# Attention output of a delta-rule block made 512 columns wide by two accumulating matmuls for each pair of heads

## The chip, the cores and the metric

The kernel runs on one core of one Trainium2 chip. The metric is device time in microseconds for one execution of the whole program. Five engines of the core work side by side, each through its own list of instructions in order, and meet at semaphores: PE multiplies matrices (its weight loads are listed apart, as PEld), DVE does vector work and transposes blocks of 32x32, ACT does activations and copies, POOL small memsets, copies and indirect transfers, SP issues transfers.

## The reference

A transformer block over 16 sequences of 512 tokens and 128 channels: layer norm with a modulation, a gated delta-rule attention with 8 heads of 16 channels, an output projection, then a mixture of 16 experts. The part that the change touches is one line of the chunked delta rule, with chunks of 32 tokens:

```python
def step(S, xs):
    q_i, k_i, u_i, w_i = xs
    attn_local = jnp.where(mask_strict, 0.0, q_i @ jnp.swapaxes(k_i, -1, -2))
    u_new = u_i - w_i @ S
    o_i = q_i @ S + attn_local @ u_new          # <- this line
    S = S + jnp.swapaxes(k_i, -1, -2) @ u_new
    return (S, o_i)
```

## The kernel before, in words

Four stages follow one another: setup, `stage_front` (projections, the delta rule, stores to DRAM), `stage_back` (filters, gates, output projection, routing) and the experts. The change is in `stage_front`.

`stage_front` walks over 26 rounds, `i` from -10 to 15, with 16 chunks of 32 tokens. A round works at several depths at once: `n = i+9` normalizes and turns the input, `t = i+5` projects k, v, q and the gates, `t4 = i+4` scales, `t3 = i+3` makes the in-chunk attention, and `d = i` runs the recurrence. So rounds 0 to 6 have all of it, rounds 7 to 10 no `n`, round 11 has `t4`, `t3` and `d`, round 12 `t3` and `d`, rounds 13 to 15 only `d`. Each engine has one list for all rounds, written out by hand and fully unrolled, and `need(engine, semaphore, n)` puts a wait into it.

The 128 partitions hold four quads of 32. A quad and a sequence make a pair of heads, so there are 64 such pairs, and `per_pair` (L562) issues one 32x32 matmul for each. PE's order in a round is: `r` (L596, state times scaled keys), the gates' spread `sm` (L600), half of k's projection, `gl` (L608), the other half, `u` (L617), half of v, `ga` (L624), half of v, `s` (L632, the state), half of q, `o1` (L639, q times state), half of q, the two fusion matmuls `f0` and `f1` (L646), `o` (L649, attention times u), the input's transposes `x` (L655) and the `dense` group (L659 to L666).

`o1` and `o` both write `ps_b`, 64 columns for each pair: the two heads of a pair beside each other, 32 tokens each, and all 32 channels of the pair for both. For head 0 only the first 16 channels mean something, for head 1 only the last 16. DVE turns all 1024 columns (L795) into `o_wide`, which is the buffer of `u_wide`; ACT's `take_valid` (L443) copies the valid halves in two activations into `o_tok`, and SP stores that (L414). The same `take_valid` makes `u_tok` from `u_wide` (L493).

What stands after the second `take_valid` in ACT's list is the modulated input `f_hT` (L552) and the copy `f_dense` (L558), and the next round's `sm` on PE waits for `f_dense`. What stands around L795 in DVE's list is the triangular solve (`part`, L681 and L684), the transposes of its result (L804, two of them in odd rounds), and then `r` of the next round (L702), `f_sm_tok` (L708) and `L` (L732); PE's `u` waits for L702 and L732.

Of the kernel before, what the change touches and what calls it, by code (L numbers as in the profile page):

```python
# [19 lines left out]
ACT = mybir.ActivationFunctionType  # L20
AXX = mybir.AxisListType.X

P = 128
NB, S, D = 16, 512, 128
NH, DH = 8, 16
C = 32
# [6 lines left out]
NQ, G2 = 4, 2  # L33
# [246 lines left out]


FIRST = -10
D_K, D_Q, D_KT, D_W, D_KG, D_T, D_A = 3, 6, 6, 5, 5, 4, 4


def need(eng, sem, n, per=1):

    if n >= 0:
        eng.wait_ge(sem, (n + 1) * per)  # L289


def unit(n):

    return n if 0 <= n < NCH else None


def stage_front(nc, g, a):


    with ExitStack() as stack:  # L300
        k = Ctx(nc, stack)
        W = NB * C
# [6 lines left out]
        q_cm = [k.sb(f"f_q_cm{u}", [P, W]) for u in range(D_Q)]  # L309
# [17 lines left out]
        TT = [TT_all[:, u, :, :, :] for u in range(D_T)]  # L327
        attn = [k.sb(f"f_attn{u}", [P, NI, C]) for u in range(D_A)]
        r = k.sb("f_r", [P, W])
        u_wide, u_tok = k.sb("f_u_wide", [P, NB * 64]), k.sb("f_u_tok", [P, W])  # L330
        o_wide = u_wide
        state = [k.sb(f"f_state{u}", [P, W]) for u in range(2)]
        o_tok = [k.sb(f"f_o_tok{u}", [P, W]) for u in range(2)]
        ps_p = [k.ps(f"ps_p{u}") for u in range(2)]
# [4 lines left out]
                   v_halo k_turned v_turned short_step short_done s_turned sm_turned sm_halved  # L339
                   nk_root nk_inv beta_ready bn_step gamma_ready kg_turned kg_ready w_ready heads_ready  # L340
                   gl_ps ga_ps L_taken attn_ready L_masked solved TT_ready
                   state_ready r_ps r_ready u_ps u_ready u_copied s_ps o1_ps o_ps o_turned o_copied fir_ready""".split()
        s = {n: nc.alloc_semaphore(name="f_" + n) for n in names}
        xs_in = [nc.alloc_semaphore(name=f"f_xs_in{u}") for u in range(3)]
        v_out, s_out, sm_out, o_out = ([nc.alloc_semaphore(name=f"f_{n}_out{u}") for u in range(2)] for n in ("v", "s", "sm", "o"))
# [1 line left out]
        quad = lambda q: slice(32 * q, 32 * q + 32)  # L347
        by_seq = lambda x: x.rearrange("p (b c) -> p b c", b=NB)
        SOLVE = 60
        every_TT = TT_all[:, :, :, :, :].rearrange("p t b i g -> p (t b i g)")  # L350
        window = every_TT[:, NB * D:].rearrange("p (c w k) -> p c w k", c=C, w=2)
        w_in = nc.alloc_semaphore(name="f_w_in")
        own.append(w_in)
        block = stack.enter_context(nc.Block())
# [29 lines left out]
        @block.sync  # L384
        def _(sp):
            def load_x(n):
                need(sp, s["xh_ready"], n - 3)
                sp.dma_start(x_in[n % 3][:, :, :], a.x[4 * (n % 4):4 * (n % 4) + 4, n // 4 * P:n // 4 * P + P, :]
                             .rearrange("b p d -> p b d")).then_inc(xs_in[n % 3], 16)

            def store(dst, t, src, sems):
                sp.dma_start(dst[t], src).then_inc(sems[t % 2], 16)

            for n in range(3):
                load_x(n)
            for q in range(NQ):
                sp.dma_start(window[quad(q), :, :, :], a.windows[q]).then_inc(w_in, 16)
            for i in range(FIRST, NCH):
                m = unit(i + 4)
                if m is not None:  # L400
                    need(sp, s["s_turned"], m)
                    store(a.s_tok, m, s_tok[m % 2][:, :], s_out)
                    need(sp, s["sm_halved"], m)
                    store(a.logits, m, sm_half[m % 2][:, :, :].rearrange("p b r -> p (b r)"), sm_out)
                t = unit(i + 5)
                if t is not None:
                    need(sp, s["v_turned"], t)
                    if t >= 3:
                        store(a.v_tok, t, v_of(t), v_out)
                n = unit(i + 12)  # L410
                if n is not None and n >= 3:
                    load_x(n)
                if unit(i) is not None:
                    need(sp, s["o_copied"], i)  # L414
                    store(a.o_tok, i, o_tok[i % 2][:, :], o_out)
            for sems in (s_out, sm_out, o_out):
                for sem in sems:
                    sp.wait_ge(sem, 16 * NCH // 2)
            for u, n in ((0, 6), (1, 7)):
                sp.wait_ge(v_out[u], 16 * n)  # L420

        @block.gpsimd
        def _(pool):
            pool.memset(state[1][:, :], 0.0).then_inc(s["state_ready"], 1)
            for i in range(FIRST, NCH):
                t, n = unit(i + 5), unit(i + 9)
                if t is not None:
                    need(pool, s["short_done"], t - 2)
                    if t == 0:
                        pool.memset(v_pad[0][:, :, 0:FIR_S - 1], 0.0).then_inc(s["v_halo"], 1)  # L430
                    else:
                        need(pool, s["silu_v"], t - 1)
                        pool.tensor_copy(v_pad[t % 2][:, :, 0:FIR_S - 1], v_pad[1 - t % 2][:, :, C:]).then_inc(s["v_halo"], 1)  # L433
                if n is not None:
                    j, rows = n // 4, slice(4 * (n % 4), 4 * (n % 4) + 4)
                    need(pool, s["dense_ps"], 4 * j - 5)
                    if j == 0:
                        pool.memset(hT[0][:, rows, 0:TAPS - 1], 0.0).then_inc(s["halo_ready"], 1)
                    else:
                        need(pool, s["h_ready"], n - 4)  # L440
                        pool.tensor_copy(hT[j % 2][:, rows, 0:TAPS - 1], hT[1 - j % 2][:, rows, P:]).then_inc(s["halo_ready"], 1)

        @block.scalar  # L443
        def _(act):
            def take_valid(out, wide):

                for n in range(G2):
                    last = act.activation(by_seq(out[:, :])[:, :, n * DH:(n + 1) * DH],
                                          by_seq(wide[:, :])[:, :, 48 * n:48 * n + DH], ACT.Copy)
                return last  # L450

            def upper_to_identity(half):
# [8 lines left out]
            for i in range(FIRST, NCH):  # L461
# [28 lines left out]
                if unit(i) is not None:  # L490
                    need(act, s["u_ready"], i)
                    need(act, s["o_ps"], i - 1)
                    take_valid(u_tok, u_wide).then_inc(s["u_copied"], 1)  # L493
                if n is not None:
                    need(act, s["ln_ready"], n)
                    need(act, s["x_ps"], n - 1)
# [40 lines left out]
                if t3 is not None:  # L537
                    need(act, s["L_taken"], t3)
                    upper_to_identity(L[t3 // 2 % 2][:, t3 % 2, :, :]).then_inc(s["L_masked"], 1)
                if unit(i) is not None:  # L540
                    need(act, s["o_turned"], i)
                    if i >= 2:
                        act.wait_ge(o_out[i % 2], 16 * (i // 2))
                    take_valid(o_tok[i % 2], o_wide).then_inc(s["o_copied"], 1)
                if n is not None:
                    need(act, s["x_ps"], n)
                    need(act, s["dense_ps"], 4 * (n // 4) - 5)
# [13 lines left out]
        def _(pe):  # L561
# [8 lines left out]
            double = lambda x: lambda b, q: x[quad(q), b * 64:b * 64 + 64]  # L570
            every = lambda b: True
            never = lambda b: False
            in_bank = lambda b: b % 8 == 0

            def u_pair(b, q):

                cols = u_wide[quad(q), b * 64:b * 64 + 64]
                return bass.AP(cols.tensor, cols.offset, [list(cols.ap[0]), [48, 2], [1, DH]])

            def project(t, kind, which, half):  # L580
                ps = free_bank(pe, kind, t) if half == 0 else ps_p[bank[kind, t]]
# [8 lines left out]
            for i in range(FIRST, NCH):  # L590
# [45 lines left out]
                if d is not None:  # L636
                    need(pe, s["attn_ready"], min(d + 3, NCH - 1))
                    need(pe, s["o_turned"], d - 1)
                    per_pair(double(ps_b), narrow(state[(d - 1) % 2]),  # L639
                             lambda b, q: q_cm[d % D_Q][quad(q), b * C:b * C + C].unsqueeze(1).broadcast_to([32, G2, C]), in_bank, stop=False)\  # L640
                        .then_inc(s["o1_ps"], 1)
                if t is not None:
                    project(t, "q", 0, 1)
                    for m in range(2):
                        ps = free_bank(pe, f"f{m}", t)
                        pe.matmul(ps[:, :], g.fus_W1[:, m * P:(m + 1) * P], tokens(t, TAPS - 1), start=True, stop=True).then_inc(s[f"f{m}_ps"], 1)  # L646
                if d is not None:
                    need(pe, s["u_copied"], d)
                    per_pair(double(ps_b), narrow(u_tok), lambda b, q: attn[d % D_A][quad(q), 2 * b:2 * b + 2, :].rearrange("p g c -> p (g c)"), never)\  # L649
                        .then_inc(s["o_ps"], 1)  # L650
                if n is not None:
                    ps = free_bank(pe, "x", n)
                    need(pe, s["xh_ready"], n)
# [16 lines left out]
        def _(dve):  # L670
# [18 lines left out]
            for i in range(FIRST, NCH):  # L689
# [66 lines left out]
                if d is not None:  # L756
                    need(dve, s["u_ps"], d)
                    need(dve, s["s_ps"], d - 1)
                    need(dve, s["u_copied"], d - 1)
                    need(dve, s["o_copied"], d - 1)  # L760
                    dve.transpose(u_wide[:, :].rearrange("p (b g z) -> p b g z", b=NB, g=G2), ps_a[:, :].rearrange("p (b i g) -> p b g i", b=NB, g=G2)).then_inc(s["u_ready"], 1)
                part(0, 3)
                if t3 is not None:
# [25 lines left out]
                part(10, 13)  # L789
                if d is not None:  # L790
                    need(dve, s["o_ps"], d)
                    need(dve, s["o_copied"], d - 1)
                    need(dve, s["s_ps"], d)
                    need(dve, s["u_copied"], d)
                    dve.transpose(o_wide[:, :], ps_b[:, :]).then_inc(s["o_turned"], 1)  # L795
                part(13, 15)
                if i % 2 == 1:
                    for m in (i + 1, i + 2):
# [680 lines left out]
```

## Time and profile before

| | |
|---|---|
| median of 3 runs | 1112.25 us (1108.51 to 1112.86) |
| the profiled execution | 1113.23 us, span 1111.5 us |
| mean granted TensorE clock | 0.852 of full |
| PE busy | 805.0 us, 72% of the span |
| weight loads busy | 497.9 us |
| DVE busy | 739.3 us, 67% |
| ACT busy | 461.1 us, 41% |
| POOL busy | 202.2 us, 18% |

Times on the page and in the rows are microseconds unless marked ns. A matmul of f32 shows as two MATMUL records and two LDWEIGHTS records, so a group of 64 pairs is "x128" of each. "Idle before, releaser" says what ended an engine's idle time; "issue" is time in which nothing that the profile shows kept the engine. The granted clock is a share of full speed.

### The profile page before, as it was taken

To read this page: it belongs to the slowest core of one execution; us is meant where nothing else is said; L and a number is where in the kernel's file an instruction comes from. 1 tells how busy PE (TensorE), PEld (TensorE's weight loads), DVE (VectorE), ACT (ScalarE), POOL (GpSimd) and SP (SyncE) were. 2 spreads that over 40 slices of the span, in tenths; PEclk is the share of its full clock that TensorE was granted. 3 is DMA by queue.
4 is the path that set the end of the run, shared out by engine and by line. 5 is a ranking of instruction groups with operands and counts; after the bars stand their busy time and mean duration, and the time that the engine had idled before them with its cause. 6 is when DMAs were issued, how large, how long until landed. Compare 5 with 4: busy or idle time off the path is not lost. (4 is left out here: it accounts for less than half of the span.)

```text
span 1111.5 us, 40970 instructions
## 1 busy us (share of the span) xinstructions
PE 805.0 (72%) x18289; PEld 497.9 (45%) x18289; DVE 739.3 (67%) x1595; ACT 461.1 (41%) x880; POOL 202.2 (18%) x227
## 2 busy tenths in 40 slices
PE   1388977989899899998655474989877156667660
PEld 1134434555455555555654473545532024444440
DVE  3143998889999899998886139899985524222320
ACT  1587665556556565554210113557566111001000
POOL 2000000000000000000000000111111057888875
PEclk9999997989999899999776766888888569778775
DMA  5200111011000101111000092344352024344432
GB/s 118 54 30 29 36 35 36 31 42 47 32 33 32 37 28 37 37 37 37 14 14 13 22 288 76 105 120 120 100 130 58 21 80 96 68 69 84 72 37 25
DMA packets 86440, 66.13 MB, mean 60 GB/s; under 512 B 18504, under 2 KB 72952, under 8 KB 86264
## 3 DMA queue, kind: packets, MB, share of 16 engines
q1 hardware_dynamic: 73580, 54.42, 17.2%
q0 software_dynamic: 11264, 8.40, 5.6%
q8 instruction: 144, 2.36, 0.9%
q10 hardware_dynamic: 1420, 0.70, 0.2%
q14 instruction: 32, 0.26, 0.1%
HBM read 36.33 MB, written 27.15 MB: 57 GB/s over the span
## 5 line engine op out<-in xcount | busy, mean ns | idle before, releaser
L586 PE MATMUL ps_p<-f_hT,Wconv 128*128 128x512 f32 x384 | 193.5, 634 | 3.3 <-ACT f_hT L552 1.6
L684 DVE TENSOR_TENSOR f_L<-f_L,f_prod 128x60 f32<-128x60 f32 (+14 forms) x240 | 121.3, 505 | 8.2
L681 DVE TENSOR_TENSOR f_prod<-f_L 128x60 f32<-128x60 f32 (+14 forms) x240 | 118.9, 495 | 6.0
L1299 POOL DMA_INDIRECT out_dram<-y,slot_row x64 | 101.1, 1580 | 27.8 <-issue 18.0
L586 PEld LDWEIGHTS ps_p<-f_hT,Wconv 128*128 128x128 f32 x384 | 70.3, 196 | 77.8 <-issue 70.0
L1348 ACT ACTIVATE act_g<-pe_g 128x512 f32<-128x512 f32 x32 | 17.4, 595 | 167.3 <-PE pe_g L1326 140.6
L433 POOL COPY f_v_pad<-f_v_pad 128x32 f32<-128x32 f32 x15 | 4.7, 311 | 418.3 <-ACT f_v_pad L515 418.3
L1316 PE MATMUL pe_x<-ident,got 128*128 128x128 f32 x64 | 15.5, 388 | 85.4 <-DMA got<-xh_dram,slot_row 85.4
L1290 POOL DMA_INDIRECT got<-xh_dram,slot_row x64 | 62.8, 982 | 57.8 <-POOLq L1179 38.6
L1377 DVE SCALAR_TENSOR_TENSOR y<-pe_y,slot_w,gb_rows 128x128 f32<-128x128 f32 x64 | 18.0, 345 | 81.7 <-DMA out_dram<-y,slot_row 74.2
L566 PE MATMUL ps_a<-f_TT,f_r 32*32 32x64 f32 x2048 | 41.9, 249 | 29.7 <-DVE f_L L732 18.0
L566 PEld LDWEIGHTS ps_a<-f_TT,f_r 32*32 32x32 f32 x2048 | 38.8, 128 | 39.3 <-issue 27.4
L1338 PE MATMUL pe_y<-w,gu 128*128 128x128 f32 x256 | 50.8, 381 | 7.2 <-DVE gu L1369 4.1
L1316 PEld LDWEIGHTS pe_x<-ident,got 128*128 128x128 f32 x64 | 10.2, 193 | 98.7 <-DMA got<-xh_dram,slot_row 97.0
L1338 PEld LDWEIGHTS pe_y<-w,gu 128*128 128x128 f32 x256 | 49.2, 295 | 8.9 <-DVE gu L1369 5.4
L1022 PE MATMUL b_ps_o<-b_WoB,b_nT 128*32 128x128 f32 x512 | 21.7, 322 | 32.7 <-DVE b_nT L1171 32.7
L1002 PE MATMUL b_ps_y<-b_v_rest,fir 32*32 32x64 f32 x768 | 42.5, 286 | 2.5 <-issue 2.5
L922 POOL TENSOR_SCALAR b_rstd<-b_mv 128x4 f32<-128x4 f32 x16 | 8.8, 548 | 189.1 <-DVE b_mv L1151 189.1
L566 PE MATMUL ps_b<-f_q_cm,f_state 32*32 32x64 f32 x2048 | 37.0, 223 | 7.9 <-issue 6.8
L1003 PE MATMUL b_ps_y<-b_v_rest,fir 32*32 32x64 f32 x768 | 42.5, 284 | 0.0
L566 PEld LDWEIGHTS ps_b<-f_q_cm,f_state 32*32 32x32 f32 x2048 | 32.8, 110 | 18.1 <-issue 16.8
L566 PE MATMUL ps_b<-f_attn,f_u_tok 32*32 32x64 f32 x2048 | 35.8, 224 | 6.4 <-issue 6.3
(247 smaller groups left out, 1792.2 us busy)
## 6 DMA issues: line engine op xcount, KB each, us to landing
w<-in_L_ffn_w_dram SPq DMA_DIRECT2D x48, 128.0 KB
f_x_in<-_attn_hidden_states_dram SPq DMA_DIRECT2D x16, 256.0 KB, 2.9
s_tok_dram<-f_s_tok SPq DMA_DIRECT2D x16, 256.0 KB, 2.1
o_tok_dram<-f_o_tok SPq DMA_DIRECT2D x16, 256.0 KB, 2.1
b_s_in<-s_tok_dram SPq DMA_DIRECT2D x16, 256.0 KB, 2.9
b_o_in<-o_tok_dram SPq DMA_DIRECT2D x16, 256.0 KB, 3.1
b_x_in<-_attn_hidden_states_dram SPq DMA_DIRECT2D x64, 64.0 KB, 2.0
out_dram<-b_x SPq DMA_DIRECT2D x64, 64.0 KB, 1.8
```

Source lines behind the costliest of these rows:

```text
L566: last = pe.matmul(out(b, q), lhs(b, q), rhs(b, q), start=start(b), stop=stop, skip_group_check=True)
L586: last = pe.matmul(ps[:, :], g.Wconv[:, which, tap, :], tokens(t, tap), start=(tap == 0), stop=(tap == TAPS - 1))
L681: dve.tensor_tensor(tmp, M[:, :, m + 1:, m:m + 1].broadcast_to([P, 2, rows, cols]), M[:, :, m:m + 1, 0:cols].broadcast_to([P, 2, rows, col ...
L684: dve.tensor_tensor(M[:, :, m + 1:, 0:cols], M[:, :, m + 1:, 0:cols], tmp, ALU.add).then_inc(s["solved"], 1)
L1002: pe.matmul(out, g.fir[quad(q), c, 1, :], now, start=True, stop=False, skip_group_check=True)
L1003: last = pe.matmul(out[:, 64 - n:], g.fir[quad(q), c, 0, :], past, start=False, stop=True, skip_group_check=True)
L1022: last = pe.matmul(ps_o[m % 2][quad(b % 4), b // 4 * D:(b // 4 + 1) * D], nT[m % 2][:, b * C:(b + 1) * C], WoB[:, b, :], start=False, stop ...
L1290: pool.indirect_dma_start(got[t % AHEAD][:, n * D:(n + 1) * D], None, flat_xh, bass.IndirectOffsetOnAxis(ap=g.slot_row[:, t, n:n + 1], axi ...
L1299: pool.indirect_dma_start(flat_out, bass.IndirectOffsetOnAxis(ap=g.slot_row[:, t, n:n + 1], axis=0), y[t % 2][:, n * D:(n + 1) * D], None, ...
L1316: last = pe.transpose(ps_x[:, n * P:(n + 1) * P], got[t % AHEAD][:, n * D:(n + 1) * D], g.ident[:, :])
L1338: last = pe.matmul(ps_y[:, n * D:(n + 1) * D], gu[:, m, n * P:(n + 1) * P], w3[u][:, m, :], start=(m == 0), stop=(m == 1))
L1377: last = dve.scalar_tensor_tensor(y[t % 2][:, n * D:(n + 1) * D], ps_y[:, n * D:(n + 1) * D], g.slot_w[:, t, n:n + 1], g.gb_rows[:, n // 2 ...
```

## The change

The output is made 512 columns wide. `o1` multiplies each pair's block-diagonal state once by q (32 columns instead of 64). `u` is copied into a zeroed buffer `u_apart` with one 32-channel block for each head of a pair, in which the other head's channels stay zero; `o` is then two matmuls of 32 columns for each pair, which accumulate. That makes 128 matmuls of `o` in place of 64; they are split in two halves, one behind `f0`, one behind `f1`. DVE turns the 512 columns straight into `o_tok`; ACT's second `take_valid` and its wait for `o_turned` go, SP waits for `o_turned`, and DVE now waits itself until the store from that `o_tok` has landed. DVE's L761 no longer waits for `o_copied`. POOL zeroes `u_apart` once at the start. The buffers of `f_TT` go from four to two; the window data of the filters, which was kept in two of them for a time, now lies in these two.

```diff
-D_K, D_Q, D_KT, D_W, D_KG, D_T, D_A = 3, 6, 6, 5, 5, 4, 4
+D_K, D_Q, D_KT, D_W, D_KG, D_T, D_A = 3, 6, 6, 5, 5, 2, 4
...
-        u_wide, u_tok = k.sb("f_u_wide", [P, NB * 64]), k.sb("f_u_tok", [P, W])
-        o_wide = u_wide
+        u_wide, u_apart = k.sb("f_u_wide", [P, NB * 64]), k.sb("f_u_apart", [P, G2, NB, C])
...
-        window = every_TT[:, NB * D:].rearrange("p (c w k) -> p c w k", c=C, w=2)
+        window = every_TT.rearrange("p (c w k) -> p c w k", c=C, w=2)
...
-                    need(sp, s["o_copied"], i)
+                    need(sp, s["o_turned"], i)
                     store(a.o_tok, i, o_tok[i % 2][:, :], o_out)
...
+            pool.memset(u_apart[:, :, :, :], 0.0).then_inc(s["zeroed"], 1)
...
-            def take_valid(out, wide):
+            def to_own_half(out, wide):
                 for n in range(G2):
-                    last = act.activation(by_seq(out[:, :])[:, :, n * DH:(n + 1) * DH],
-                                          by_seq(wide[:, :])[:, :, 48 * n:48 * n + DH], ACT.Copy)
+                    cols = slice(n * DH, (n + 1) * DH)
+                    last = act.activation(out[:, n, :, cols], by_seq(wide[:, :])[:, :, 48 * n:48 * n + DH], ACT.Copy)
...
-                if unit(i) is not None:
-                    need(act, s["o_turned"], i)
-                    if i >= 2:
-                        act.wait_ge(o_out[i % 2], 16 * (i // 2))
-                    take_valid(o_tok[i % 2], o_wide).then_inc(s["o_copied"], 1)
...
+            def own_attention(d, first, end):
+                for b in range(first, end):
+                    for n2 in range(G2):
+                        for q in range(NQ):
+                            last = pe.matmul(ps_b[quad(q), b * C:b * C + C], u_apart[quad(q), n2, b, :], attn[d % D_A][quad(q), 2 * b + n2, :],
+                                             start=False, stop=(n2 == 1), skip_group_check=True)
+                if end == NB:
+                    last.then_inc(s["o_ps"], 1)
...
-                    per_pair(double(ps_b), narrow(state[(d - 1) % 2]),
-                             lambda b, q: q_cm[d % D_Q][quad(q), b * C:b * C + C].unsqueeze(1).broadcast_to([32, G2, C]), in_bank, stop=False)\
-                        .then_inc(s["o1_ps"], 1)
+                    per_pair(narrow(ps_b), narrow(state[(d - 1) % 2]), narrow(q_cm[d % D_Q]), at_first, stop=False).then_inc(s["o1_ps"], 1)
...
+                    if d is not None:
+                        need(pe, s["u_copied"], d)
+                        own_attention(d, NB // 2 * m, NB // 2 * (m + 1))
...
-                    need(dve, s["o_copied"], d - 1)
-                    need(dve, s["s_ps"], d)
-                    need(dve, s["u_copied"], d)
-                    dve.transpose(o_wide[:, :], ps_b[:, :]).then_inc(s["o_turned"], 1)
+                    if d >= 2:
+                        dve.wait_ge(o_out[d % 2], 16 * (d // 2))
+                    dve.transpose(o_tok[d % 2][:, :], ps_b[:, 0:W]).then_inc(s["o_turned"], 1)
```

## Rows read from the trace of the kernel before

**Rows 1.** The page: DMA queues (packets, MB, share of 16 engines).
```profile
q8 instruction: 144, 2.36, 0.9%
```

**Rows 2.** Windows by stage: us, then busy us (count) of PE, PEld, DVE, ACT, POOL, granted clock, DMA.
```profile
174.57:376.20 201.63, 184.97 (x5640) 109.90 (x5640) 178.96 (x363) 116.74 (x238) 2.75 (x12) 0.94 0.11 38
376.20:523.96 147.76, 140.21 (x4677) 84.98 (x4677) 139.22 (x249) 84.44 (x162) 1.27 (x4) 1.00 0.10 34
523.96:639.20 115.24, 66.35 (x3456) 61.97 (x3457) 69.65 (x117) 16.05 (x47) 0.02 (x1) 0.72 0.05 17
...
243.51:275.22 31.71, 29.21 (x941) 17.63 (x941) 28.47 (x59) 19.94 (x41) 0.41 (x2) 1.00 0.11 35
```

**Rows 3.** Timeline at the end of round 3: start, us, engine line op, [idle before, releaser].
```profile
296.93 1.24 DVE L795 STREAM_TRANSPOSE f_u_wide<-ps_b 128x1024 f32<-128x1024 f32 x1
298.20 0.72 ACT L448 ACTIVATE f_o_tok<-f_u_wide 128x256 f32<-128x256 f32 x2 [3.15 <-DVE f_u_wide L795]
...
300.20 0.60 ACT L558 ACTIVATE f_dense<-ps_p 128x512 f32<-128x512 f32 x1
...
300.95 1.95 PE L600 MATMUL ps_p<-f_dense,spread 128*128 128x512 f32 x2 [3.40 <-ACT f_dense L558]
...
302.94 0.72 DVE L708 STREAM_TRANSPOSE f_sm_tok<-ps_p 128x512 f32<-128x512 f32 x1 [0.80 <-PE ps_p L600]
...
304.23 0.18 DVE L712 RECIPROCAL f_rstd<-f_dev 128x4 f32<-128x4 f32 x1 [0.58 <-ACT f_dev L474]
```

**Rows 4.** Groups by line: busy us, mean ns, then idle before.
```profile
L795 DVE STREAM_TRANSPOSE f_u_wide<-ps_b 128x1024 f32<-128x1024 f32 x16 | 19.9, 1244 | 19.8 <-PE ps_b L566 19.8
...
L728 DVE STREAM_TRANSPOSE f_s_tok<-f_short 128x512 f32<-128x512 f32 x16 | 11.4, 711 | 0.6
...
L448 ACT ACTIVATE f_o_tok<-f_u_wide 128x256 f32<-128x256 f32 x32 | 11.6, 410 | 67.1 <-DVE f_u_wide L795 67.1
```

**Rows 5.** Timeline of PE in round 4.
```profile
316.91 1.29 PE L566 MATMUL ps_s<-f_u_wide,f_k_tok 32*32 32x32 f32 x128
...
320.37 1.56 PE L586 MATMUL ps_p<-f_hT,Wconv 128*128 128x512 f32 x3 [1.55 <-issue]
...
326.25 1.98 PE L646 MATMUL ps_p<-f_hT,fus_W 128*128 128x512 f32 x4
328.16 1.99 PE L566 MATMUL ps_b<-f_attn,f_u_tok 32*32 32x64 f32 x128
```

**Rows 6.** Windows from one "issue" stall of PE to the next, rounds 12 to 15.
```profile
562.95:566.70 3.75, 1.99 (x129) 1.83 (x129) 3.54 (x7) 0.00 (x0) 0.00 (x0) 1.00 0.02 4
...
sum 26.31, PE 14.22 PEld 12.99 DVE 12.88 ACT 0.72 POOL 0.00; mean PE 2.03 PEld 1.86 DVE 1.84 ACT 0.10 POOL 0.00
```

**Rows 7.** Windows of round 8, cut after every 256 instructions of PE's list.
```profile
441.07:444.52 3.45, 3.45 (x142) 2.11 (x135) 2.84 (x6) 2.32 (x4) 0.00 (x0) 1.00 0.02 5
444.52:447.93 3.41, 3.41 (x150) 2.12 (x140) 3.27 (x8) 1.56 (x4) 0.22 (x1) 1.00 0.22 82
447.93:453.47 5.54, 5.54 (x142) 3.06 (x134) 5.23 (x10) 2.36 (x3) 0.00 (x0) 1.00 0.01 3
453.47:456.89 3.42, 3.42 (x143) 1.85 (x133) 3.32 (x5) 2.43 (x9) 0.00 (x0) 1.00 0.02 5
```

**Rows 8.** Timeline, rounds 11 to 15: what PE's `u` waits for, and DVE and ACT there.
```profile
547.27 1.02 PE L566 MATMUL ps_a<-f_heads_k,f_k_cm 32*32 32x64 f32 x57 [0.79 <-issue]
...
549.80 1.23 DVE L732 STREAM_TRANSPOSE f_L<-ps_a 128x1024 f32<-128x1024 f32 x1
...
551.28 0.97 PE L566 MATMUL ps_a<-f_TT,f_r 32*32 32x64 f32 x28 [2.99 <-DVE f_L L732]
...
574.97 1.29 PE L566 MATMUL ps_a<-f_TT,f_r 32*32 32x64 f32 x40 [3.35 <-DVE f_r L702]
...
599.95 1.29 PE L566 MATMUL ps_a<-f_TT,f_r 32*32 32x64 f32 x40 [7.19 <-DVE f_r L702]
...
634.90 0.72 ACT L448 ACTIVATE f_o_tok<-f_u_wide 128x256 f32<-128x256 f32 x2 [9.10 <-DVE f_u_wide L795]
```

More of the change, by code:

```diff
@@ L341, in stage_front @@
                    gl_ps ga_ps L_taken attn_ready L_masked solved TT_ready
-                   state_ready r_ps r_ready u_ps u_ready u_copied s_ps o1_ps o_ps o_turned o_copied fir_ready""".split()
+                   state_ready r_ps r_ready u_ps u_ready u_copied zeroed s_ps o1_ps o_ps o_turned fir_ready""".split()
         s = {n: nc.alloc_semaphore(name="f_" + n) for n in names}
@@ L492, in _ @@
                     need(act, s["o_ps"], i - 1)
-                    take_valid(u_tok, u_wide).then_inc(s["u_copied"], 1)
+                    need(act, s["zeroed"], 0)
+                    to_own_half(u_apart, u_wide).then_inc(s["u_copied"], 1)
                 if n is not None:
@@ L572, in _ @@
             never = lambda b: False
-            in_bank = lambda b: b % 8 == 0
+            at_first = lambda b: b == 0
             def u_pair(b, q):
@@ L638, in _ @@
                     need(pe, s["o_turned"], d - 1)
-                    per_pair(double(ps_b), narrow(state[(d - 1) % 2]),
-                             lambda b, q: q_cm[d % D_Q][quad(q), b * C:b * C + C].unsqueeze(1).broadcast_to([32, G2, C]), in_bank, stop=False)\
-                        .then_inc(s["o1_ps"], 1)
+                    per_pair(narrow(ps_b), narrow(state[(d - 1) % 2]), narrow(q_cm[d % D_Q]), at_first, stop=False).then_inc(s["o1_ps"], 1)
                 if t is not None:
                     project(t, "q", 0, 1)
-                    for m in range(2):
+                for m in range(2):
+                    if t is not None:
                         ps = free_bank(pe, f"f{m}", t)
                         pe.matmul(ps[:, :], g.fus_W1[:, m * P:(m + 1) * P], tokens(t, TAPS - 1), start=True, stop=True).then_inc(s[f"f{m}_ps"], 1)
[L647 to L650, printed above, removed]
+                    if d is not None:
+                        need(pe, s["u_copied"], d)
+                        own_attention(d, NB // 2 * m, NB // 2 * (m + 1))
                 if n is not None:
@@ L791, in _ @@
                     need(dve, s["o_ps"], d)
-                    need(dve, s["o_copied"], d - 1)
-                    need(dve, s["s_ps"], d)
-                    need(dve, s["u_copied"], d)
-                    dve.transpose(o_wide[:, :], ps_b[:, :]).then_inc(s["o_turned"], 1)
+                    if d >= 2:
+                        dve.wait_ge(o_out[d % 2], 16 * (d // 2))
+                    dve.transpose(o_tok[d % 2][:, :], ps_b[:, 0:W]).then_inc(s["o_turned"], 1)
                 part(13, 15)
```

## The prediction, made before the changed kernel ran

> **What bounds the kernel now.** I read the windows by stage first, then the end of one round on all engines, then PE alone.
>
> The stretch that the change touches runs from the first `u` of the recurrence to the start of the back stage. It has three parts [rows 2]: rounds 0 to 5, 33.6 us each (201.63 over 6); rounds 6 to 10, 29.55 us each (147.76 over 5); and a tail of 115.24 us, rounds 11 to 15 and the way out. In the first two parts PE is busy 92 and 95% and DVE 89 and 94%. Two in-order lists, both nearly full, wait for each other in a ring, so a gain on one counts only as far as the other allows. In the tail both are half idle, and the time is a chain.
>
> The end of round 3 shows how the ring costs PE time [rows 3]. ACT stands 3.15 us idle until DVE comes to L795, behind the solve. Then follow the copies into `f_o_tok`, `f_hT`, `f_dense`, and only then `sm`, which has left PE idle for 3.40 us. DVE in turn waits 0.80 us at L708 for `sm`, which here ran at a low clock (1.95 us). The granted clock over rounds 0 to 5 is 0.94, over round 2 alone 1.00, and round 2 is 1.9 us shorter than the mean of the six [rows 2].
>
> PE alone shows a second limit, and this decides my forecast. In the tail it stops for "issue" again and again, and from one such stop to the next lie 256 of its instructions (128 matmul records, 128 weight loads) each time: seven such windows take 26.31 us, 3.76 each, with 2.03 us of matmul in them [rows 6]. The instruction queue moved 144 packets in 2.36 MB, 16 KB each [rows 1]. I read this as code that comes in pages of 256 instructions; two page starts in a row lie 3.76 us apart when PE has nothing else to wait for. In full rounds a page is hidden when other work fills it. In round 8 the pages of the second half take 3.45, 3.41, 5.54 and 3.42 us [rows 7], with no stall; in round 4, stalls of 1.55 us and less do show [rows 5].
>
> **The change part by part.** *Matmuls.* `o1` turns from 64 to 32 columns: 1.99 becomes 1.29, the duration of `s` in that shape [rows 5], so -0.70 us. `o` becomes two such groups, 2.58 for 1.99: +0.59. The fusion pair (1.91 us from its start to that of `o`) is cut in two, which adds one change between full-size and small matmuls; no row shows a pair cut so. Between 0 (the pair without overhead) and 0.3 I take 0.2. PE's arithmetic therefore stays as it is, +0.1 us a round.
>
> *Instructions.* 64 more matmuls are 128 more records and 128 weight loads: exactly one more page in each of 16 rounds, all of it in the second half of the round, where pages already came at 3.4 us.
>
> The Trainium skill (Runtime: NRT & Kernel Launch, section Instruction fetch mechanics) says that code is refilled in 16 KiB blocks of 256 instructions while the current one runs, and that crossing a boundary is "mostly hidden". The block size agrees with this trace (2.36 MB in 144 packets); that it is hidden does not hold in the tail, where 1.7 us of 3.76 are idle. By the page the new block would cost nothing, which is the second rival below.
>
> *ACT.* The second `take_valid` (2 x 0.41 us) and the wait for L795 go [rows 4]. What is late next on that chain is `dense` on PE, which is done before `r`; so `sm` follows `r` at once, and PE's idle stretches of up to 3.4 us and the low clock behind them go. `f1` is later by half of `o`, and its gelu with it; that is hidden, because `dense` comes behind the other half.
>
> *DVE.* L795 turns half the columns: 1244 to 711 ns [rows 4], -0.53 a round. Its waits for `sm` (0.80) shrink. The new wait for the store two rounds back is hidden: that store was issued two rounds earlier. SP's wait changes its semaphore only, and what stands behind it is the next round's stores. POOL's memset stands at the head of a list that is busy for 4 us of these three parts [rows 2]; its first reader comes ten rounds later. The wait of `f_TT` for `u` two chunks back asks for what DVE has consumed by then at L761. These I take at 0; the TT wait would cost up to the 2.4 us of two L804s in each second round if that were wrong.
>
> **The sum, by stage.**
>
> *Rounds 0 to 5.* Round 2, without low clock, has PE busy for 29.2 us [rows 2]. To that come 0.1 and the stalls of the extra page. The pages of the second half (3.41, 5.54, 3.42, so 12.4 us [rows 7]) become four pages, which at 3.76 are 15.0: +2.6, or at 3.4 (the shortest that shows no stall) 13.6, +1.2; I take 2.0. PE then needs 31.3. DVE is busy 29.8 a round (178.96 over 6); less 0.53, plus what lies between its 60 instructions (363 over 6 rounds; 0.03 us each is my estimate from neighbouring starts, 1.8 together) and the 0.58 us that L712 waits for ACT [rows 3], which stays, it needs 31.7. Odd rounds have two L804s (2.4 us) and even ones none, and the ring takes the longer at each turn, so I add 0.4: 32.1 against 33.6, -1.5 a round, **-9 us**. Bounds: -1.9 a round if DVE's sum alone counts (-11), -0.5 if PE's stalls come on top of DVE's odd rounds (-3).
>
> *Rounds 6 to 10.* There is little idle time to win back. PE is busy 28.0 of 29.55 us, and the extra page adds 1.2 to 2.6; less the small stalls that exist I take +1.7 a round, **+8.5 us**. Bounds: -0.5 (DVE's shorter transpose alone, -2.5 in all) to +2.6 (+13).
>
> *Tail.* Here the page is bare, 3.76 us in each round, unless DVE hides it. Round 11: `gl` ends at 548.29 and `L` can be turned from 549.80, so 1.5 are hidden [rows 8]: +2.25. Round 12: PE then waits 3.35 us until L702 has run, of which some 0.7 is L702 itself; `r` therefore comes late by 3.76 - 2.6: +1.15. Round 13: PE waits 7.19 us for DVE, which hides the page, and DVE is 0.53 shorter: -0.5. Round 14 waits for nothing but code (0.79 us for L702 itself, behind `r`): +3.76. Round 15: +3.76. At the way out the 0.53 and the last copy (0.72) go: -1.25. Together **+9.2 us**; bounds +5 (pages at 3.4, more of it hidden) and +13 (nothing hidden in rounds 11 and 12).
>
> Back stage and experts are not touched. Sum: -9 + 8.5 + 9.2 = +8.7. The profiled execution took 1113.23 us (1.7 of it around the span); the median of the runs is 1 us below. I forecast 1121 us beside that median, own range 1114 to 1129.
>
> **Rivals.** *The page is hidden (faster).* Place: the second half of each round. If a page can start less than some 3.0 us after the one before it as soon as PE has work, 12.4 us hold four pages and no stall comes. Then rounds 0 to 5 give -1.9 each (-11), rounds 6 to 10 -0.5 each (-2.5), and the tail -1.25 and -0.5: -15, so 1097 us. For it: page starts 3.41 apart without a stall [rows 7]. Against it: seven windows in a row at 3.76 [rows 6], and a stall in round 4 in just this place, where one page holds `s` and half of q [rows 5]. The quoted page of the skill speaks for this rival; the rows of the tail speak against it.
>
> *A balance.* Gain and loss cancel: rounds 0 to 5 at -1.9, rounds 6 to 10 at +0.2 (the stalls lie under DVE's own work), tail +9: -11 + 1 + 9 = -1, so about 1111 us. For it: DVE and PE are so close that a small shift decides which one is late.
>
> *The clock falls.* With three pages of `o` in a row PE works some 2.2 us of each 3.76. In the tail the granted clock is 0.72 over all [rows 2], and 1.00 in a window of 3.75 us with 1.99 us of matmul [rows 6]. Should it fall from 2.4 to 1.2 GHz behind `o`, `x` and `dense` (2.4 us) take twice as long in 11 rounds: +26, so about 1147 us. Against it: it stayed at 1.00 in windows as thin as this.
>
> **How the numbers follow.** Forecast 0.52, page hidden 0.18, balance 0.22, clock 0.08. A measurement of this kernel tells about 0.5% from no change, 5.6 us: below 1106.7 is faster, above 1117.8 slower. Of the forecast 0.08 lies below that upper line, of the hidden page 0.02 above the lower one. Slower: 0.44 + 0.08 = 0.52; same: 0.22 + 0.08 + 0.02 = 0.32; faster: 0.16. The range of 1106 to 1133 holds the forecast and the balance and leaves out most of the hidden page and the clock, 0.2 together.
>
> **What would show it.** PE's idle time before `sm` by `f_dense` gone in rounds 0 to 6, and ACT no longer idle by L795. Rounds 0 to 5 near 32 us, 6 to 10 near 31, the tail near 124. Between `f0` and `r`, "issue" stalls of 1 to 2 us in every round, 256 instructions apart; 160 packets of code instead of 144. The prediction is wrong if the groups behind `f0` follow each other without such stalls, if rounds 6 to 10 don't grow, or if rounds 14 and 15 grow by less than 3 us each.

## The result, and the profile after

The changed kernel takes 1124.31 us (median of 4 runs, 1118.85 to 1127.85) against 1110.38 us for the kernel before on the same chip: a ratio of 1.0126, 95% interval 1.0069 to 1.0183. It is slower by 14 us (by the interval 8 to 20), where 1121 against 1112.25 (+9) was forecast, and inside the range.

The three parts of the front stage in the profiled execution of the changed kernel, from its first `u` to the start of the back stage (columns as in rows 2):

```profile
174.01:368.44 194.43, 177.90 (x6408) 106.87 (x6409) 174.97 (x362) 115.05 (x228) 2.57 (x12) 0.99 0.12 38
368.44:528.26 159.82, 142.14 (x5317) 85.16 (x5318) 138.40 (x250) 80.19 (x150) 1.65 (x4) 1.00 0.10 33
528.26:650.60 122.34, 68.65 (x4097) 64.22 (x4098) 67.22 (x117) 12.38 (x37) 0.04 (x1) 0.60 0.05 17
```

Beside [rows 2]: rounds 0 to 5 went from 201.63 to 194.43 us (-7.2), rounds 6 to 10 from 147.76 to 159.82 (+12.1), the tail from 115.24 to 122.34 (+7.1). Together +12.0. The part behind, which the change does not touch, took 472.3 us in the profile of before and 466.1 here; over the nine profiles of this study it lies between 466 and 476, so a single span says little about 6 us, and the windows say it better. Of the four executions the profiled one was the fastest, 1118.85 us.

PE's waits at lines of the front stage, over the whole execution, first of the kernel before, then of the changed one (who waited, for what: us in all, times, longest):

```profile
PE ps_p L600 <- ACT f_dense L558: 17.7, 12, 3.4
PE ps_b L566 <- issue: 13.1, 12, 1.9
PE ps_r L566 <- issue: 10.0, 6, 2.2
```
```profile
PE ps_b L581 <- issue: 29.7, 21, 2.2
...
PE ps_b L562 <- issue: 12.3, 12, 2.2
PE ps_r L562 <- issue: 12.1, 11, 2.2
...
PE ps_p L606 <- ACT f_dense L554: 3.6, 4, 1.0
```

That is the exchange in these lines: 14 us of waiting for `f_dense` gone (what is left, 3.6 us, lies ahead of the first `u`), 31 us of "issue" come. L566 holds `o1` and `o` together; of its 13.1 us 6.3 were at `o`, so the new `o` (L581) has 23 of the 31. With the smaller groups PE's "issue" waits grow by 9.2 us in rounds 0 to 5 (3.0 to 12.2), by 11.3 in rounds 6 to 10 (4.1 to 15.4) and by 14.6 in the tail (23.7 to 38.3). In rounds 0 to 5 the `f_dense` waits that went were 12.9 us; that these rounds are shorter all the same goes with PE's busy time, 177.90 us for 184.97, at a granted clock of 0.99 for 0.94.

The gain is seen at the end of round 3 of the changed kernel, first on PE, then on ACT, where [rows 3] had `sm` 3.40 us late:

```profile
293.57 1.09 PE L562 MATMUL ps_r<-f_state,f_kg_cm 32*32 32x32 f32 x105 [0.22 <-issue]
294.59 1.13 PE L606 MATMUL ps_p<-f_dense,spread 128*128 128x512 f32 x2
295.55 1.88 PE L592 MATMUL ps_p<-f_hT,Wconv 128*128 128x512 f32 x4
```
```profile
291.22 1.51 ACT L548 ACTIVATE f_hT<-ps_p,mod 128x128 f32<-128x128 f32 x4 [1.34 <-PE ps_p L659]
293.07 0.60 ACT L554 ACTIVATE f_dense<-ps_p 128x512 f32<-128x512 f32 x1 [0.35 <-PE ps_p L670]
```

ACT is never behind DVE here: `f_dense` waits only for PE, `sm` follows `r` at once and runs at full clock (1.13 us at a granted 1.00, for 1.95 at 0.53).

The loss is seen in round 9, on PE alone:

```profile
476.04 1.17 PE L562 MATMUL ps_b<-f_q_cm,f_state 32*32 32x32 f32 x114 [0.43 <-issue]
477.14 1.99 PE L592 MATMUL ps_p<-f_hT,Wconv 128*128 128x512 f32 x4
478.97 1.02 PE L651 MATMUL ps_p<-f_hT,fus_W 128*128 128x512 f32 x2
479.92 1.29 PE L581 MATMUL ps_b<-f_attn,f_u_apart 32*32 32x32 f32 x128
481.14 1.13 PE L651 MATMUL ps_p<-f_hT,fus_W 128*128 128x512 f32 x2
482.20 0.26 PE L581 MATMUL ps_b<-f_attn,f_u_apart 32*32 32x32 f32 x6
483.26 1.24 PE L581 MATMUL ps_b<-f_attn,f_u_apart 32*32 32x32 f32 x122 [0.80 <-issue]
...
486.73 1.90 PE L670 MATMUL ps_p<-f_hid,small_w 128*32 128x512 f32 x4 [1.25 <-issue]
488.56 1.24 PE L562 MATMUL ps_r<-f_state,f_kg_cm 32*32 32x32 f32 x123
490.84 0.25 PE L562 MATMUL ps_r<-f_state,f_kg_cm 32*32 32x32 f32 x5 [1.04 <-issue]
```

PE stops inside a group (after 6 of 128 records of `o`, after 123 of 128 of `r`), with nothing to wait for by its program. The starts behind these stops, 476.04, 483.26, 486.73 and 490.84, have 512, 256 and 256 instructions between them: 7.22 us for two pages, then 3.47 and 4.11 for one each. The times of the single packets in the trace tie these stops to code: a 16 KB packet of the instruction queue ends 1.2 us before the start at 483.26 and 1.4 us before those at 486.73 and 490.84. In [rows 7] the pages of this half of a round held 3.41 to 5.54 us of matmul and none of them stopped PE. The page of the profile now counts 160 packets of code:

```profile
q8 instruction: 160, 2.62, 1.0%
```

### The profile page after: what moved, and what is told of

The parts are those of the page before. It is cut to its first block and busy times, and to the rows that moved or that the text cites. A ratio compares the mean times of both kernels' runs of the same rounds, so it can differ in the third digit from the quotient of the medians.

```text
span 1116.7 us, 44992 instructions
## 1 busy us (share of the span) xinstructions
PE 797.5 (71%) x20337; PEld 495.6 (44%) x20337; DVE 731.6 (66%) x1595; ACT 451.0 (40%) x848; POOL 202.6 (18%) x228
## 5 line engine op out<-in xcount | busy, mean ns | idle before, releaser
L592 PE MATMUL ps_p<-f_hT,Wconv 128*128 128x512 f32 x384 | 187.1, 616 | 4.0 <-issue 2.2
L592 PEld LDWEIGHTS ps_p<-f_hT,Wconv 128*128 128x128 f32 x384 | 68.0, 190 | 74.1 <-issue 66.6
L581 PE MATMUL ps_b<-f_attn,f_u_apart 32*32 32x32 f32 x4096 | 50.9, 206 | 29.7 <-issue 29.7
L581 PEld LDWEIGHTS ps_b<-f_attn,f_u_apart 32*32 32x32 f32 x4096 | 45.5, 118 | 48.9 <-issue 48.9
L449 ACT ACTIVATE f_u_apart<-f_u_wide 128x256 f32<-128x256 f32 x32 | 11.6, 408 | 122.9 <-DVE f_u_wide L764 122.9
L1318 PEld LDWEIGHTS pe_x<-ident,got 128*128 128x128 f32 x64 | 10.5, 197 | 98.8 <-DMA got<-xh_dram,slot_row 97.0
L1024 PE MATMUL b_ps_o<-b_WoB,b_nT 128*32 128x128 f32 x512 | 21.7, 322 | 30.8 <-DVE b_nT L1173 30.7
```

Source lines behind the costliest of these rows:

```text
L581: last = pe.matmul(ps_b[quad(q), b * C:b * C + C], u_apart[quad(q), n2, b, :], attn[d % D_A][quad(q), 2 * b + n2, :], start=False, stop=(n ...
L592: last = pe.matmul(ps[:, :], g.Wconv[:, which, tap, :], tokens(t, tap), start=(tap == 0), stop=(tap == TAPS - 1))
L1024: last = pe.matmul(ps_o[m % 2][quad(b % 4), b // 4 * D:(b // 4 + 1) * D], nT[m % 2][:, b * C:(b + 1) * C], WoB[:, b, :], start=False, stop ...
L1318: last = pe.transpose(ps_x[:, n * P:(n + 1) * P], got[t % AHEAD][:, n * D:(n + 1) * D], g.ident[:, :])
```

## The experiments

The stage times below are from the profile of each kernel, cut at its own `u` of rounds 0, 6 and 11 and at the start of the back stage. Ratios are to the kernel before, which ran on the same chip; its median was 1110.38 us beside the changed kernel and 1108.31 or 1109.87 beside the experiments, so differences of medians between comparisons are good to some 2 us.

**One page less, all other edits kept.** The changed kernel, but `o` for one head only (the kernel leaves out the second head's attention).

```diff
-                    for n2 in range(G2):
+                    for n2 in range(1):
...
-                                             start=False, stop=(n2 == 1), skip_group_check=True)
+                                             start=False, stop=True, skip_group_check=True)
```

> The changed kernel with `o` for the first head of each pair only (the second head's attention is left out of the output): 64 matmuls of 32 columns, so one code page a round less, and all other edits kept. Theory (the extra page of 256 instructions sets the time): rounds 0 to 5 from 32.4 to about 31.3 us each, rounds 6 to 10 from 32.0 to 29.2, the tail from 122.3 to about 114; 1102 us, some 22 below the changed kernel and below the kernel before. Rival A (the extra matmuls' own time, 1.2 us a group where nothing hides it): 10 to 15 below the changed kernel, no faster than before. Rival B (the new waits and the order set the time, not the count): within 4 us of the changed kernel.

Measured: 1096.42 us, ratio 0.9923 (0.9893 to 0.9952).

```profile
173.11:364.79 191.68, 174.41 (x5641) 103.24 (x5642) 174.31 (x362) 113.52 (x228) 2.89 (x12) 0.97 0.12 38
364.79:510.68 145.89, 136.72 (x4677) 79.74 (x4677) 136.68 (x250) 79.96 (x150) 1.30 (x4) 0.99 0.10 36
510.68:622.32 111.64, 59.74 (x3456) 55.47 (x3457) 66.92 (x117) 12.43 (x37) 0.04 (x1) 0.61 0.05 18
```

Rounds 6 to 10 fall by 13.9 us against the changed kernel and the tail by 10.7, rounds 0 to 5 by 2.8. A round takes 31.9, then 29.2 us, where the theory had 31.3 and 29.2, and the tail is 2 us shorter than it had. Without the second group the kernel is some 8 us below the kernel before by the ratio (11.9 by the medians), but it also has less to compute: its `o` is one group of 32 columns (1.29 us) where the kernel before has one of 64 (1.99 us). The second group costs 28 us by the medians, 27 by the windows, 22 by the two ratios. Sixteen such groups at their own 1.2 us are 19 us if nothing hid any of it; 13.9 us in five rounds, 2.8 each, is more than they can take. The "issue" waits of rounds 6 to 10 are back at 3.9 us. This alone does not say yet that it is code.

**The page alone, in the kernel before.** 64 matmuls of one column behind the old `o`, into the bank that the next `r` overwrites.

```diff
+                    per_pair(lambda b, q: ps_r[quad(q), b * C:b * C + 1], narrow(u_tok), lambda b, q: attn[d % D_A][quad(q), 2 * b, 0:1], every)
```

> The kernel before with one more group of 64 matmuls of a single column behind `o` in each round of the recurrence, into a bank that the next `r` overwrites: one code page more, nothing else changed, so ACT's wait for the turned output stays. Theory (code page): tail +8, rounds 6 to 10 +9 to +10, rounds 0 to 5 +3 to +9; 1130 to 1137 us. Rival A (own time of the group, at most 1.2 us): about +3 in the tail, +3 in rounds 6 to 10, 1116 to 1119 us. Rival B: no change, 1110.

Measured: 1137.37 us, ratio 1.0256 (1.0228 to 1.0284): the sum is at the upper end of the theory, 18 us and more above both rivals.

```profile
173.41:377.96 204.55, 189.34 (x6408) 115.46 (x6409) 178.45 (x362) 117.30 (x239) 2.35 (x12) 0.96 0.11 37
377.96:543.63 165.67, 151.86 (x5316) 92.42 (x5317) 140.69 (x250) 84.53 (x162) 1.66 (x4) 0.97 0.09 32
543.63:664.15 120.52, 71.42 (x4097) 66.81 (x4097) 69.79 (x117) 16.04 (x47) 0.04 (x1) 0.73 0.05 17
```

Rounds 6 to 10 grow by 17.9 us, the tail by 5.3, rounds 0 to 5 by 2.9, where much of it fell into PE's wait for `f_dense` (12.9 us before, 1.2 here). The parts are not those of the theory, which had 9 to 10 and 8 for the first two: the sum is right in part by luck. Nor is the group free: its 64 matmuls of one column keep PE busy for 1.4 us, 7.0 us in rounds 6 to 10, more than the 1.2 that was expected. What is left there, 10.9 us, goes with 7.5 us more of "issue" and a clock of 0.97 for 1.00. So in these rounds a group of little work, without any other edit, costs well over its own time. The sum does not say that: over all three parts the groups are busy for 24.6 of the 26.1 us.

**A second extra page.** The changed kernel with the same one-column group behind `o`.

```diff
+                if d is not None:
+                    per_pair(lambda b, q: ps_r[quad(q), b * C:b * C + 1], lambda b, q: u_apart[quad(q), 0, b, :], lambda b, q: attn[d % D_A][quad(q), 2 * b, 0:1], every)
```

> The changed kernel with one more group of 64 matmuls of a single column behind `o`, into the bank of the next `r`: a second extra code page. Theory (PE's list is at the rate of its code, about 3.75 us a page, in the second half of every round): the whole page is added, 3 to 3.75 us in 11 full rounds and in four of the five tail rounds; 1124 + 45 to 56, so 1169 to 1180 us. Rival A (own time of the group, 1.2 us at most): +13 to +19, 1137 to 1143 us. Rival B (the first extra page was a one-off loss of alignment): within 6 us of the changed kernel.

Measured: 1193.62 us, ratio 1.0747 (1.0707 to 1.0787), which is 69 us above the changed kernel: further out than the theory had it, and far from both rivals. The added groups are busy for 29.6 us in the three parts, so their own time is less than half of it.

```profile
173.82:399.10 225.28, 199.49 (x7176) 119.19 (x7177) 175.41 (x362) 114.19 (x227) 2.22 (x12) 0.91 0.10 34
399.10:581.57 182.47, 159.35 (x5957) 94.76 (x5958) 138.61 (x250) 81.34 (x152) 1.65 (x4) 0.92 0.09 30
581.57:719.24 137.67, 79.50 (x4736) 74.31 (x4737) 67.46 (x117) 12.45 (x37) 0.04 (x1) 0.58 0.05 15
```

The tail grows by 15.3 us, which is four pages at 3.8. The full rounds grow by 5.1 (0 to 5) and 4.5 (6 to 10) each, more than a page. What goes with it is the granted clock, 0.91 and 0.92 where the changed kernel has 0.99 and 1.00. In rounds 0 to 5 PE is busy for 21.6 us more, of which the added group is 10.5; the other 11.1, 1.8 a round, are the old matmuls taking longer. Without them a round grows by 3.3, near a page. That the added page brought the clock down is likely, but was not tried by itself.

**`o` in one piece.** The changed kernel with `f0` and `f1` together ahead of all of `o`.

```diff
-                for m in range(2):
-                    if t is not None:
+                if t is not None:
+                    for m in range(2):
                         ps = free_bank(pe, f"f{m}", t)
...
-                    if d is not None:
-                        need(pe, s["u_copied"], d)
-                        own_attention(d, NB // 2 * m, NB // 2 * (m + 1))
+                if d is not None:
+                    need(pe, s["u_copied"], d)
+                    own_attention(d, 0, NB)
```

> The changed kernel with `o` in one piece behind both fusion matmuls. Theory (page starts lie at least 3.5 to 3.8 us apart): the page with half of q and both fusion matmuls takes 5 us and hides nothing further, the two pages of `o` stand bare at 3.75 each, so about +1 us in each of 11 rounds, 1132 to 1137 us, tail unchanged. Rival A (the cut itself costs, one more change between large and small matmuls): -2 us, 1122. Rival B: no change.

Measured: 1137.02 us, ratio 1.0257 (1.022 to 1.0294), 13 above the changed kernel, at the upper end of the theory.

```profile
174.45:381.16 206.71, 186.78 (x6408) 110.09 (x6409) 175.62 (x362) 113.95 (x227) 2.19 (x12) 0.93 0.11 36
381.16:547.26 166.10, 145.03 (x5317) 85.60 (x5318) 138.50 (x250) 81.14 (x152) 1.66 (x4) 0.97 0.09 32
547.26:670.20 122.94, 67.70 (x4096) 62.85 (x4097) 67.28 (x117) 12.42 (x37) 0.04 (x1) 0.61 0.05 17
```

The same instructions and the same matmuls in another order are 12.3 and 6.3 us longer in the full rounds, and equal in the tail (122.94 against 122.34), where nothing lies between them. Two things make up the difference. The "issue" waits grow by 6.0 and 3.7 us, some 1 us a round, as the theory had it. And PE is busy for 8.9 and 2.9 us more, at a clock of 0.93 and 0.97: the low clock comes behind `o`, where the `dense` group stands. Its first matmuls in rounds 0 to 5 (one line each from the changed kernel, this one and the one with a second extra page; the last figures are busy us and the mean ns of one):

```profile
L663 PE MATMUL ps_p<-f_hT,small_w 128*32 128x512 f32 x12 | 6.3, 605 | 0.0
L663 PE MATMUL ps_p<-f_hT,small_w 128*32 128x512 f32 x12 | 9.8, 910 | 0.0
L665 PE MATMUL ps_p<-f_hT,small_w 128*32 128x512 f32 x12 | 11.5, 1061 | 0.0
```

So here, with the large matmuls spread between the small ones, more of the code is hidden and the clock stays up; the cut that I had priced as a cost (0.2 us a round) saves over 1 us. How much of that the clock alone would cost was not tried.

**Two buffers of `f_TT` alone.** The kernel before with that part of the change.

```diff
-D_K, D_Q, D_KT, D_W, D_KG, D_T, D_A = 3, 6, 6, 5, 5, 4, 4
+D_K, D_Q, D_KT, D_W, D_KG, D_T, D_A = 3, 6, 6, 5, 5, 2, 4
...
-        window = every_TT[:, NB * D:].rearrange("p (c w k) -> p c w k", c=C, w=2)
+        window = every_TT.rearrange("p (c w k) -> p c w k", c=C, w=2)
```

> The kernel before with two buffers of `f_TT` instead of four, that part of the change alone. Theory (its wait asks for what DVE has consumed already): no difference, within 4 us of the kernel before. Rival (the two transposes of each second round wait for `u`): up to +2.4 us in 8 rounds, +19.

Measured: 1109.12 us, ratio 0.9992 (0.9965 to 1.0019): no difference within 0.35%, as priced, and far from the rival's 19 us. Its three parts in the profile, 198.47, 149.34 and 113.49 us, also show by how much one execution of an equal schedule differs from another: 3.2, 1.6 and 1.8 us.

**The gain without the page.** The kernel before with ACT's copy of the turned output behind `f_dense`.

```diff
+                    act.activation(dense[:, :], ps_p[bank["dense", t]][:, :], ACT.Copy).then_inc(s["dense_ready"], 1)
                 if unit(i) is not None:
                     need(act, s["o_turned"], i)
                     if i >= 2:
                         act.wait_ge(o_out[i % 2], 16 * (i // 2))
                     take_valid(o_tok[i % 2], o_wide).then_inc(s["o_copied"], 1)
...
-                    act.activation(dense[:, :], ps_p[bank["dense", t]][:, :], ACT.Copy).then_inc(s["dense_ready"], 1)
```

> The kernel before with ACT's copy of the turned output moved behind `f_dense` in ACT's list: the wait that `sm` inherits goes, with no instruction more on PE and DVE's wide transpose kept. Theory (what the change won in rounds 0 to 5 is this wait): rounds 0 to 5 from 33.6 to about 32.3 us each, rounds 6 to 10 and the tail as before; 1101 to 1104 us. Rival (the gain came from DVE's half-size transpose, since DVE is full): rounds 0 to 5 unchanged, 1110.

Measured: 1104.45 us, ratio 0.9967 (0.9947 to 0.9987).

```profile
175.16:369.50 194.34, 178.68 (x5641) 109.67 (x5641) 177.60 (x362) 117.95 (x240) 2.32 (x12) 0.97 0.11 38
369.50:523.79 154.29, 144.57 (x4676) 87.39 (x4677) 139.59 (x250) 83.06 (x160) 1.21 (x4) 0.98 0.10 34
```

Rounds 0 to 5 take 194.34 us (32.4 each), the same as in the changed kernel, and 4.1 to 7.3 below the two profiles with the early copy (198.47 and 201.63); the wide transpose is still there, and no `f_dense` wait is left. So the wait of `sm`, with the clock that rose with it (0.97), is what was won there, and the rival falls; DVE's shorter transpose may show where PE is relieved too (191.68 with one page less), within what one profile can tell. In all it is less than I expected: 3.9 us below the kernel before in its comparison, where 6 to 9 were due. This one profile has rounds 6 to 10 at 154.29, 6.5 longer than before; it is of the longest execution of the twelve (1112.44 us), so it says little about these rounds.

**The copy in the next round.** To see whether the late copy held DVE up, it went behind the small copy for the logits, where ACT waits for k anyway.

```diff
                     act.activation(sm_half[t % 2][:, :, :], sm_tok[t % 2][:, :, 0:16], ACT.Copy).then_inc(s["sm_halved"], 1)
+                if unit(i - 1) is not None:
+                    need(act, s["o_turned"], i - 1)
+                    if i - 1 >= 2:
+                        act.wait_ge(o_out[(i - 1) % 2], 16 * ((i - 1) // 2))
+                    take_valid(o_tok[(i - 1) % 2], o_wide).then_inc(s["o_copied"], 1)
```

> The kernel before with ACT's copy of the turned output moved into the next round, behind the small copy for the logits, where ACT stands idle before k's activation. Theory (code pages and the two full lists bound the round; the copy only has to be out of the way of `f_dense`): rounds 0 to 5 about 32.3 us each as with the copy behind `f_dense`, rounds 6 to 10 about 29.5, tail unchanged; 1098 to 1104 us, no slower than the copy behind `f_dense`. Rival (a late copy holds up L761, which waits for it): rounds 6 to 10 and the tail grow, 1106 to 1112 us.

Measured: 1107.21 us, ratio 0.9969 (0.9938 to 1.0): the same gain as with the copy behind `f_dense`, 0.9967. Its parts are 194.34, 150.78 and 113.19 us. The absolute time lies inside the rival's 1106 to 1112 and above the theory's 1098 to 1104, so the theory missed. The parts do not bear the rival out either: the tail did not grow (115.24 before), and rounds 6 to 10 are 3.0 us longer than before, where equal schedules differ by 1.6. Whether a late copy holds DVE up stays open. The interval of the copy behind `f_dense` lies clear of 1, 0.3% below the kernel before, and that of this one reaches 1; the two are not told apart from each other.

## Why the prediction was right, step by step

*The page of code.* It is the step that decided the sign, and it holds: 16 more packets, stops at 256 instructions with a packet's end 1.2 to 1.4 us before PE goes on, and added pages that cost more than their own matmuls, the second one more than twice as much. Windows between stops in round 14, two of the kernel before and three of the changed one, beside 3.76 us in [rows 6]:

```profile
609.37:613.12 3.75, 1.99 (x129) 1.83 (x128) 0.00 (x0) 0.00 (x0) 0.00 (x0) 1.00 0.02 4
613.12:616.70 3.58, 1.66 (x128) 1.55 (x127) 1.25 (x1) 0.72 (x2) 0.00 (x0) 1.00 0.02 5
...
615.98:619.46 3.48, 1.30 (x130) 1.20 (x129) 0.00 (x0) 0.00 (x0) 0.00 (x0) 0.67 0.02 5
619.46:622.94 3.48, 1.93 (x129) 1.80 (x129) 0.00 (x0) 0.00 (x0) 0.00 (x0) 0.50 0.02 5
622.94:626.80 3.86, 1.93 (x129) 1.79 (x128) 0.72 (x1) 0.00 (x0) 0.00 (x0) 0.50 0.20 72
```

*Rounds 0 to 5.* Forecast 32.1 us each and -9; measured 32.4 and -7.2. The wait by `f_dense` went as told and the clock rose from 0.94 to 0.99. DVE waited 8.9 us for PE over these rounds, 1.5 each, for which the sum had left 0.4.

*Rounds 6 to 10.* Forecast +8.5 with a bound of +13; measured +12.1. This is the term that I sized too small. I let the stalls of four pages at 3.76 us count 1.2 to 2.6 us a round and took 1.7; the "issue" waits grew by 2.3 a round and the round by 2.4. DVE now waits for PE there, 15.5 us over the five rounds (2.7 before), 4.4 of it in four of them ahead of the transpose of `o`, as in round 8:

```profile
454.31 0.72 DVE L797 STREAM_TRANSPOSE f_o_tok<-ps_b 128x512 f32<-128x512 f32 x1 [0.79 <-PE ps_b L581]
```

so DVE's own gain of 0.53 us is worth nothing in these rounds: PE with its code is the bound.

*Tail.* From `u` to `u`, and from the last `u` to the back stage: 27.32, 23.69, 24.98, 18.30, 20.97 us before, 29.86, 24.99, 24.43, 21.16, 21.90 after. The differences +2.5, +1.3, -0.6, +2.9, +0.9 stand against +2.25, +1.15, -0.5, +3.76 and +2.5 (3.76 - 1.25). The three rounds with DVE's slack came out almost exactly. The last two were forecast too long, and by the prediction's own sign (wrong if rounds 14 and 15 grow by less than 3 us each) this step failed: they grew by 2.9 and 0.9, or 2.2 without the way out. The page itself came as priced. In round 14 three windows of 10.82 us stand where two took 7.33, +3.49; but the stretch ahead of the first stop is 0.97 shorter (`s` took 1.29 us there for 1.93) and that behind the last 0.35 longer. For round 15, PE before, then after:

```profile
627.71 1.14 PE L566 MATMUL ps_b<-f_q_cm,f_state 32*32 32x64 f32 x66 [1.86 <-issue]
...
631.45 2.13 PE L566 MATMUL ps_b<-f_attn,f_u_tok 32*32 32x64 f32 x67 [1.00 <-issue]
```
```profile
637.57 1.11 PE L562 MATMUL ps_b<-f_q_cm,f_state 32*32 32x32 f32 x66 [1.10 <-issue]
...
641.59 1.93 PE L581 MATMUL ps_b<-f_attn,f_u_apart 32*32 32x32 f32 x128 [2.09 <-issue]
645.06 1.17 PE L581 MATMUL ps_b<-f_attn,f_u_apart 32*32 32x32 f32 x67 [1.54 <-issue]
```

Two windows of 7.49 us stand where one took 3.74, +3.75, and the way out gave 1.27 back, as priced at 1.25. What the sum left out is that the rest of the chain got shorter: the piece of `o` behind the last stop (1.17 us against 2.13) and 0.59 us ahead of the first one.

*The sum.* The misses of the three parts, in the measured time +1.8, +3.6 and -2.1 us beside the forecast, partly cancel; that +8.7 came within 3.3 us of the windows' +12.0 is in part luck.

*The edits priced at nothing* (`f_TT`, POOL, the store's wait) cost nothing that shows; `f_TT` was run alone, the other two only as part of kernels. *The cut of the fusion pair* was priced with the wrong sign.

*The rivals.* The hidden page (the first rival in the list) is refuted by the stops themselves, by the page taken away and by the second page. The sentence of the Trainium skill that the cost of a boundary is mostly hidden (Runtime: NRT & Kernel Launch, section Instruction fetch mechanics) does not hold here: PE's "issue" waits in this stretch went from 30.8 to 65.9 us with one page more a round. The falling clock did not come in the full rounds of the changed kernel (1.00 in rounds 6 to 10), but the prediction dismissed it too easily. Of the seven windows behind [rows 6] three were below 1.00 (0.94, 0.74, 0.64). One page more went with 0.97 for 1.00 in rounds 6 to 10 of the kernel before, `o` in one piece with 0.93 in rounds 0 to 5, a second page with 0.91 there, and it showed where the rival had placed it, in the `dense` group behind `o`. In the tail the clock fell from 0.72 to 0.60, and to 0.61 with the page taken away, but not with the page added to the kernel before (0.73): there it goes with the narrow form and not with the page.

Open: how the 12 us in the windows and the 14 us of the medians go together was not settled; the untouched part behind differs by up to 10 us between executions, and the front stage by some 2 to 3 us in each of its parts.

## What to carry to other kernels

Where small matmuls follow each other, count instructions as well as columns: 64 f32 matmuls were one 16 KB page of code, and the starts of two bare pages lay some 3.5 to 4.0 us apart in rounds 14 and 15 whatever their matmuls took. Look for stops inside a group of equal instructions with "issue" as the releaser, count the instructions between two such stops, try large matmuls spread evenly between the small ones, and look at the granted clock of what stands behind the stops. Before you narrow a tile to shorten a copy, see whether the wait that the copy causes can be moved instead; here one block further down in ACT's list gave the same gain in rounds 0 to 5 without a page.

## What was not expected

The cut of `o` in two halves is worth 13 us (1137.02 against 1124.31) by order alone, part of it through the clock. And the second extra page cost more than the first in full rounds, 5.1 us each in rounds 0 to 5, with the granted clock down to 0.91.
